# Unread bf16 products between the products of TensorE, in all stages of an eight-layer chain

## The reference

```
x = x + mamba(ln(x))           # two directions, 256 channels, 16 states each
x = x + moe16(ln(x))           # 16 experts of 64, 2 chosen, one shared
x = x + attention(ln(x))       # 16 heads of 64, relative bias, softmax
x = x + lora_moe(ln(x))        # 8 experts of rank 16
x = x + attention(ln(x))       # 16 heads of 8, rotary positions, causal ("attn2")
x = x + block(ln(x))           # inside: attention of 16 heads of 8, not causal ("attn3"), 8 experts of 512
x = x + memory(ln(x))          # a linear recurrence over time, per head an 8 x 8 state
x = x + moe8(ln(x))            # 8 experts of 256, gated
```

## Time and profile before

| | |
|---|---|
| median of 3 runs | 5807.99 us |
| profiled execution | 5812.37 us, span 5810.6 us |
| mean granted clock | 0.844 |
| busy: PE, DVE, ACT, POOL | 77%, 65%, 53%, 20% |
| one round of the loop | 716.8 us |

### The profile page before, as it was taken

How to read it: one execution, slowest core, us unless ns; L and a number is a source line. 1 busy time by engine, 2 the same in 40 slices (tenths; PEclk the granted TensorE clock), 3 DMA queues, 4 the chain that set the end, 5 groups by cost and what they waited for, 6 DMA issues and landing times. The chain is left out here.

```text
span 5810.6 us, 67170 instructions
## 1 busy us (share of the span) xinstructions
PE 4485.7 (77%) x20516; PEld 2226.2 (38%) x20516; DVE 3772.0 (65%) x8877; ACT 3064.0 (53%) x5351; POOL 1140.3 (20%) x1356
## 2 busy tenths in 40 slices
PE   5786778877788777887778777788778877788777
PEld 2342434424344243442434324343243433444334
DVE  6756586565865658656686556865668555686554
ACT  3365645556455555555655556555565555555443
POOL 2401132011320123201231012310123111231100
PEclk8996989978898788987889878897789987899778
DMA  4210021100210002100121001210012100121000
GB/s 160 87 36 1 21 65 55 32 1 25 67 55 26 1 28 71 52 22 1 34 73 47 20 1 37 75 48 13 1 42 75 46 11 1 44 73 47 7 1 2
DMA packets 104076, 218.53 MB, mean 38 GB/s; under 512 B 11072, under 2 KB 19776, under 8 KB 103152
## 3 DMA queue, kind: packets, MB, share of 16 engines
q1 hardware_dynamic: 103680, 213.81, 11.6%
HBM read 211.08 MB, written 2.69 MB: 37 GB/s over the span
## 5 line engine op out<-in xcount | busy, mean ns | idle before, releaser
L859 POOL TENSOR_TENSOR slot_work<-slot_work,slot_c_all 128x512 f32<-128x512 f32 x448 | 570.2, 1273 | 1015.9 <-DVE slot_work L942 1015.0
L777 PE MATMUL BANKS<-slot_work,WF 128*128 128x512 f32 x896 | 530.5, 679 | 5.7 <-DVE slot_du L918 2.9
L524 ACT ACTIVATE attn_prob<-BANKS 128x512 f32<-128x512 f32 (+3 forms) x896 | 401.5, 532 | 122.5 <-PE BANKS L426 119.0
L1000 PEld LDWEIGHTS BANKS<-WF,slot_x_a 128*128 128x128 f32 x2688 | 359.3, 197 | 264.5 <-ACT slot_x_a L1040 133.5
L1000 PE MATMUL BANKS<-WF,slot_x_a 128*128 128x128 f32 x2688 | 373.3, 283 | 86.3 <-ACT slot_x_a L1040 86.3
L1010 PE MATMUL BANKS<-XT,WF 128*128 128x512 f32 x768 | 425.3, 639 | 2.6 <-ACT slot_comb_t L306 2.6
L769 PE MATMUL BANKS<-slot_bcs,WB 96*128 96x512 bf16 x448 | 189.1, 422 | 305.1 <-DVE slot_work L942 304.0
L202 POOL TENSOR_TENSOR rstd<-rstd,WF 128x4 f32<-128x4 f32 x40 | 40.3, 1007 | 1572.7 <-DVE rstd L220 1559.5
L1809 DVE CUSTOM_DVE_ANT_0 attn_biased<-BANKS,attn_toep 128x512 f32<-128x512 f32 x448 | 306.0, 684 | 51.9 <-PE BANKS L1707 46.6
L1788 ACT COPY attn_probt<-BANKS 128x512 f32<-128x512 f32 x448 | 261.0, 583 | 147.3 <-PE BANKS L1714 144.4
L426 PE MATMUL BANKS<-attn_parts_kT,attn_parts_qT 64*128 64x512 bf16 (+3 forms) x896 | 309.2, 437 | 33.6 <-ACT attn_parts_qT L504 20.7
(11 more groups left out here) (674 smaller groups left out, 9464.7 us busy)
## 6 DMA issues: line engine op xcount, KB each, us to landing
slot_c_all<-c_rows SPq DMA_DIRECT2D x448, 256.0 KB, 3.1
attn_toep<-bias_line SPq DMA_DIRECT2D x112, 448.0 KB, 4.4
first_c_all<-c_rows SPq DMA_DIRECT2D x64, 256.0 KB, 3.1
WF<-in_wf SPq DMA_DIRECT2D x4, 1964.0 KB, 16.2
zattn_toep<-bias_line SPq DMA_DIRECT2D x16, 448.0 KB, 4.3
WF<-in_wf SPq DMA_DIRECT2D x3, 800.0 KB, 17.2
WF<-in_wf SPq DMA_DIRECT2D x3, 785.5 KB, 6.0
XIN<-in_x SPq DMA_DIRECT2D x8, 256.0 KB, 2.9
```

The lines of the kernel that those rows point to most:

```text
L524: nc.scalar.activation(prob[:, i % PR, lo:hi], bank("T", i), ACT.Exp).then_inc(exped, 1)
L777: nc.tensor.matmul(SUM, ident, work[:, m % RW, :], start=(n == 0), stop=(n == NS - 1)).then_inc(acc, 1)
L859: nc.gpsimd.tensor_tensor(work[:, m % RW, :], work[:, m % RW, :], c_all[:, m % RC, :], ALU.mult).then_inc(rd, 1)
L1000: last = nc.tensor.matmul(DOWN[e % 2][:, j * D:(j + 1) * D], a1[:, i % 3, j * P:(j + 1) * P], w_down[:, i * D:(i + 1) * D], start=(t == 0 ...
```

## The change

A helper issues `n` bf16 products of the identity with its own first column, 128 rows by 128 columns of the array and 512 columns moving, into a bank whose content nobody reads before it is written again:

```
+    def idle_products(bank, n):
+        for _ in range(n):
+            nc.tensor.matmul(bank, ident_b, bc(ident_b[:, 0:1], [P, SEQ]), start=True, stop=True)
```

More of the change, by code:

```diff
@@ L161, in _ @@
         def _(pe):
+            idle_products(PS[3], 4)
             for s in sems[1::5]:
@@ L247, in _ @@
                 def _(pe):
+                    idle_products(PS[5], 8)
                     for j in range(NJ):
@@ L251, in _ @@
                         nc.tensor.transpose(bank[:, j * P:(j + 1) * P], dst[:, j, :], ident).then_inc(turned, 1)
+                    idle_products(PS[5], 3)
                 @block.scalar
@@ L423, in score @@
                     bank_free(pe, (kind, i))
+                    idle_products(PS[slot[kind, i]], int(kind == "S" or i >= N - LAG))
                     tile, rows = i % PER // GH, slice(HS * (i % 2), HS * (i % 2 + 1))
@@ L590, in norm_parts @@
     def norm_parts(st, tag, src, dst, small, at, dst_t=None, banks=None, rms=False, sq=None, gain_t=None, gain=None,
-                   shift=None, after=None):
+                   shift=None, after=None, spare=None, idle=0):
         s_stats, s_mv, s_rstd = small
@@ L647, in tensor @@
                 return
+            if idle:
+                yield at - 1.0
+                idle_products(spare, idle)
             yield at + 3.6
@@ L768, in tensor @@
                     row = WBF("pick", 96)[:, n:n + 1]
+                    idle_products(DRIVE[s % 3], 1)
                     nc.tensor.matmul(DRIVE[s % 3], bc(row, [96, P]), bcs[:, d, :], start=True, stop=True).then_inc(b_cast, 1)
@@ L1012, in tensor @@
                     last.then_inc(hid, 1)
+                    if i == 2:
+                        idle_products(DOWN[1], 12)
                     last = nc.tensor.matmul(place("gate", i), w_gate[:, i * P:(i + 1) * P], XT[:, :], start=True, stop=True)
@@ L1128, in tensor @@
                         pe.wait_ge(cp, NJ)
+                        idle_products(PS[7], 16)
                     if i == 1:
@@ L1278, in last_layers @@
         Y = st.sb("Y", [P, NJ, D])
-        ln1 = norm_parts(st, "ln1", XN, Y, SMALL, 0.0, dst_t=XT, banks=(PS[5], PS[4]), gain=W("g1"), shift=W("be1_2"))
+        ln1 = norm_parts(st, "ln1", XN, Y, SMALL, 0.0, dst_t=XT, banks=(PS[5], PS[4]), gain=W("g1"), shift=W("be1_2"),
+                         spare=PS[7], idle=10)
         comb2, comb2_t = st.sb("comb2", [P, NJ, E2]), st.sb("comb2_t", [E2, SEQ])
@@ L1288, in last_layers @@
         ln2 = norm_parts(st, "ln2", Y, XN, SMALL, 73.0, gain=W("g2"), shift=W("be2_2"))
-        ln3 = norm_parts(st, "ln3", XO, XN, SMALL, 79.0, dst_t=XT, banks=(PS[5], PS[4]), after=(freed, 1))
+        ln3 = norm_parts(st, "ln3", XO, XN, SMALL, 79.0, dst_t=XT, banks=(PS[5], PS[4]), after=(freed, 1), spare=PS[4], idle=20)
         shared = ExitStack()
@@ L1292, in last_layers @@
             memo = memory_parts(Box(st, shared), ln3.ready, XO, Y, 84.0)
-        ln4 = norm_parts(st, "ln4", XO, XN, SMALL, 132.0, dst_t=XT, banks=(PS[5], PS[4]), after=(memo.added, 1))
+        ln4 = norm_parts(st, "ln4", XO, XN, SMALL, 132.0, dst_t=XT, banks=(PS[5], PS[4]), after=(memo.added, 1),
+                         spare=PS[7], idle=8)
         shared = ExitStack()
@@ L1838, in _ @@
                                          start=(j == 0), stop=False, skip_group_check=True)
+                    idle_products(PS[3], 12)
                     pe.wait_ge(gated, 1)
@@ L1904, in _ @@
                                          start=True, stop=True).then_inc(pj, 1)
+                    idle_products(PS[5], 40)
                 @block.scalar
```

## The result

The changed kernel takes 6260.66 us (median of 4 runs, 6250.66 to 6272.39) where the kernel before takes 5807.9 beside it: a ratio of 1.078 (95% interval 1.0758 to 1.0799), 453 us slower. Ratios go by the executions within 1.5% of the quickest of their kernel, which leaves out one of ten in e1 (10767 us), one of ten in e7 (10831 us) and two of four in e3. The forecast was 5979 us, 171 slower, with a range up to 6060. The direction was right and the size wrong by more than half.

What follows compares the result with a forecast made beforehand. TensorE's low clock was taken to cost most in attn2 and attn3, 188 of 717 us. Terms 18.4 + 7.2 - 4.2 gave +21.4 us a round, +171 over eight, so 5979 us; range 5790 to 6060, the forecast's own 5900 to 6040.

Steps and rivals of the forecast that it cites:

- The price of a product: attn3's steps 20 to 63 at 2.4 GHz: unread 0.215, gap 0.09, score 0.215, T 0.215, gap 0.09, together 0.83 us.
- attn3 before step 20: attn3's start: qkv products -1.3, interleaved steps -2.8, the turns ahead -0.8, together -4.9 us; the 40 products add 0.
- steps 20 to 63: attn3's middle steps, the main term: TensorE binds at 2.4 GHz, 50.0 us against 32.5 now, +17.5.
- attn2: Small-head attention: steps 20 to 63 +8.5, last 20 +2.9, before step 20 -4.2, together +7.2 us a round.
- Norms and moe0: Norm products at the lower clock cost about +0.5 us each norm, +1.8 a round; moe0 itself gains, -0.5.
- The blocks of 10, 20, 16, 8 and 12: Slot: these unread products stand in waits; the slot in all was put at 0 (-5 to +8).
- The price of the spreads: Slot: one unread product costs 0.215 us; 24 dense steps cost at most 5, taken as +2.
- the cover of the three banks: Slot: the three banks cover the spreads' delay except at 4 DVE waits; without cover all 64 would show, 13.8 us.
- attn1 and lora1: Two stages gain by the higher clock: attn1 -4 us (0 to -5), lora1 -1.5.
- The first: Rival, all stages: unread products ride free in TensorE's waits and the clock pays, -21 a round, 5640 us; chance 0.13.
- the second: Rival, both attentions: pairs are lost but gaps hidden, each of 64 steps 0.18 less, 5795 us; chance 0.15.
- the third: Rival, slot: it pays for the spreads' products in full, seven times +13.8, 6076 us; chance 0.07.

Runs made afterwards that it cites:

- e1: The changed kernel without the unread products ahead of scores and T's: 5799.91 us, 0.9981 of the kernel before.
- e7: The changed kernel without products ahead of scores and T's, and with 54 instead of 40 behind the qkv products in attn2 and attn3: 5807.61 us, 0.9986.
- e3: The changed kernel with 54 instead of 40 products behind the qkv products: 6238.4 us median of four; ratio of the two quicker runs 1.0634.
- e8: The changed kernel with 128 instead of 512 columns in each unread product ahead of a score or T: 6488.67 us, 1.1151.
- e11: The changed kernel with as many unread products, but in steps 20 to 63 ahead of the T instead of the score: 6160.25 us, 1.0602.
- e4: The changed kernel with each unread score product only on the 64 rows that its score uses: 5908.36 us, 1.0173.
- e10: e9 with 54 instead of 40 products behind the qkv products in attn3 alone: 5738.36 us, 0.987.
- e12: e10 with 8 unread products ahead of the output projection that ends each slot: 5728.46 us, 0.9854.
- e5: e6 also without the 8 and 3 products of moe0's norm and the 4 at a stage's end: 5759.58 us, 0.9907.
- e9: e5 without the 12 products ahead of the slot's third gate product: 5737.24 us, 0.986.
- e6: e1 also without the unread products ahead of the spreads of B: 5793.69 us, 0.9966.

## Why the forecast missed

**The price of a product: right.** Product, border, score, T, border was put at 0.83 us a step and measured 0.86. Columns, borders and lost pair are each shown by a run of its own: e8 took away three quarters of the columns and saved 0.17 us, e11 brought the pair back and saved 0.22, e4 kept the other half of the rows free and took the late 16 steps to 13.6 us. From the last score to the stage's end attn3 grew by 28.0 - 22.3 = 5.7 (+5.8 forecast), and the part ahead of the first reduction shrank from 24.0 to 21.8, 2.2 less (2.1 forecast). Two small slips of the sum change little: the interleaved step's own terms make 0.83 us and not 0.85, and ten products with the values, 1.0 and a second gap of 0.09 each, make 10.9 and not 10.5.

**attn3 before step 20: the step that failed.** The prediction put it so: the 40 products cover the wait of 11.17 us, the clock rises in the qkv products, and "an interleaved step now is turn 0.22, unread 0.215, gap, score 0.215, gap, that is 0.85 for 1.08". The 40 were sized at the level that they themselves bring about, 8.6 us; they end 2.46 us ahead of the turns, the clock falls soon after, and the steps run at the lower level, 1.5 us each and not 0.85. So what failed is the level of the clock that the steps were priced at; that the idle 2.46 us bring it down isn't shown, as the next paragraph says. These 20 steps take 29.3 us; the forecast had 15.9, and a round of e3 that held took 17.8. I expected in that case 5 us a round more; I had priced the old steps at the lower clock, not the new ones, which carry 0.54 us of product each. Steps 0 to 19 grew by 10.6 where -2.8 was forecast: 13.4 us a round.

**It doesn't end at step 20.** The prediction used 2.4 GHz for steps 20 to 63. The clock stayed low until 1359.7, and the 44 steps took 53.5 us against 31.1: +22.4, where +17.5 was forecast. The 13.4 and these 4.9 are the 18 us that attn3 lacked in a round, and most of the 157 that it lacked in all. The rounds of e3 in which the clock held show 114.5, with 132.6 where it fell: that the clock alone makes this difference is shown, in one kernel. What decides between the two in a given round is open. It isn't just the idle time ahead of the turns, since e3 has 0.30 us there in all eight rounds and falls in five, and e8 stays low without a gap in the record. The clock records of e3, e7, e10 and e12, all with 54 products in attn3, show a difference: in the 23 rounds that fell the clock had risen 3.0 to 4.4 us after the stage's start, in the nine that held it rose after 4.4 to 5.4 us or had not been low at all. That goes together with the course; that it causes it isn't shown.

**attn2: the same.** +13.9 a round for +7.2; TensorE is idle for 2.12 us ahead of its turns. The rounds at 103.6 us have the clock low for 14 us; the one at 113.4 has 41. The best of e3 is 101.1, for the forecast's 99.

**Norms and moe0: cost where a gain was forecast.** In moe0 the 8 products start only 0.9 us after the norm, which lets them run past the wait, and by the timeline the faster start opens a later wait in which the clock falls: +29 for -4, and e5 gives it back whole. In attn3 the transposes start 3.1 us after the norm (3.0 before), so there the norm's term was too high.

**The slot: right for the spreads, wrong for a block.** "The blocks of 10, 20, 16, 8 and 12 stand in waits" does not hold for the 12. In the trace of e5 the DVE instruction that follows waits 5.64 us for the gate product behind them, 2.68 before. Without them e9 is 22 us faster, of which its slots show 10 (2487.6 us for 2497.7). The price of the spreads, +2 a slot, holds: e1 against e6 gives 1 by the totals and 2 by the slots. By these two, and by the slot's rise of 4 us where 13.8 were its whole price, the cover of the three banks held.

**attn1 and lora1: right.** -2.9 a round for -4, and -1.3 for -1.5.

**The rivals.** None took place. The first, that products ride free, is refuted by the late steps, the second by the borders of 0.11 us, and the third by the slot, +4 us and not +13.8. The Trainium skill's rule in "TensorE: Matmul & The Clock Gate", "Part 3: Packing small matmuls", that a weight load overlaps only where the row group differs, was the prediction's reason for the borders, and the trace bears it out only in part. A 64-row product right behind one on the other half starts within 0.01 us of it (e11), and every border between a 128-row and a 64-row product shows (e8). But a T follows its score on the same 64 rows, with other weights, after 0.22 us, the columns alone (and 1378.62 to 1378.84 above), and in the slot a 128-row product follows the 96-row spread after 0.23. By the rule both should show a border. The timeline of the weight loads (PEld) has the two cases side by side, the load of a score behind an unread product and that of its T:

```profile
1378.61 0.09 PEld L435 LDWEIGHTS BANKS<-attn_parts_kT,attn_parts_qT 64*128 64x128 bf16 x1 [0.23 <-issue]
1378.63 0.10 PEld L435 LDWEIGHTS BANKS<-attn_qm,attn_parts_kT 64*128 64x128 bf16 x1
```

The first begins only 0.01 us ahead of its product, the second 0.21 ahead, while the score on the same rows runs. So the load of 0.1 us shows where 64 and 128 rows change over, and hides on the same 64 rows: the border's price was right, the reason given for it was not the whole one. Why the load is late at a change of rows is open.

## What to carry to other kernels

An unread product pays only in a wait of TensorE. Price it at both levels of the clock: the 40 were shorter than their wait at the upper level and would have been longer at the lower. Filling that wait to its end was worth nothing here (54 for 40 in e7 and e10), so it is no remedy by itself. Don't put a full-array product between small products that share the array by rows: here it cost its columns, two borders and the partner of the next product. If a forecast rests on a clock level, price the new instruction list at the other level too, since a slower list can also stay there for longer (126.3 us at a stretch in e8). Here the blocks in the waits alone, as e12 has them, are worth 1.5%, and each of the others had to be taken out by itself to see what it cost.

## What the runs showed of the hardware

- TensorE can be busy in every microsecond of the record and stay at 1.2 GHz: 71.00 of 71.00 us in e8, inside a stretch of 126.3. Borders count as busy in this record.
- At 2.4 GHz the product behind a bf16 product of 512 columns starts 0.22 us after it on the same 64 rows with other weights, 0.31 to 0.33 us after it where 64 and 128 rows change over, and at most 0.01 us after it on the other half of the rows.
- One list of instructions has two courses. attn3 in e3 took 114.5 to 115.2 or 132.6 us in the same execution, by whether the clock fell.
- Fewer columns in each unread product made the kernel slower, 6489 against 6261 us, though each was cheaper where the clock was up.
- A stage that starts faster can end later: moe0 rose from 40.2 to 44.4 us, its mean clock in the first 20 us 0.85 where it was 0.69.
